# Regrouping the half-height cross matmuls and recoding ahead in a fused Perceiver layer

## The chip, the cores and the metric

The kernel runs on one core of a Trainium2 chip. The metric is the device time of one execution in microseconds (us). Before the change the median of three runs is 612.24 us (612.08 to 613.53).

## The reference, cut to what matters

```python
# x: (16, 64, 1024), ctx: (16, 1024, 1024), all float32
q1 = fake_quant(layernorm(x));  q2 = fake_quant(ctx)     # codes 0..255, scale 8/255, zero 128
x = x + q1 @ q2                                          # "cross": 64x1024 by 1024x1024 for each batch
x = x + out_proj(attention(layernorm(x)))                # qkv 1024 -> 3072, 32 heads of 32, rope, causal softmax
x = x + ffn(layernorm(x))                                # W.T plus 16 rank-16 updates, merged into one matrix
```

## The kernel before, in words

The 16 batches are worked in eight pairs of 2 x 64 = 128 rows. A pair's stage on the engines is `next_pair(i)`, and it does two things at once: the qkv projection, attention and output projection of pair i, and the cross product of pair i + 1. Pairs 0 and 1 have forms of their own (`first_pair`, and `next_pair` with `late`); pairs 2 to 6 run one body, and pair 7 has no cross left. No planner is at work: the order on each engine is written out by hand, every engine is strictly in order, and semaphores tie them together.

The cross of a pair reads 16 blocks of the context, called chunks here (8 of each batch, 128 x 1024 float32, 512 KB). A chunk passes through these hands:

- **SP** loads it (`load_chunk`, L679) into one of three float32 buffers, `slots`: `raw` 0, `raw` 1 and `lnt`. `lnt` is also where the normalised rows of norm2 stand until TensorE has turned them (`x_turn`), so a chunk can go there only afterwards (the wait on `s_xt`). Chunk c has slot c % 3. Each load waits for the coding of the chunk that had the slot.
- **ACT** codes it (`quantise`, L378) to bytes in the ring `code` of eight places, place c % 8. It waits for the load, and for TensorE (`s_cmm`) and POOL (`s_acc`) to be done with the chunk eight before.
- **POOL** adds the code words of all chunks of a pair, whose column sums TensorE needs for the zero point (`add_codes`, L811; two instructions for each chunk, for pairs 3 to 7).
- **DVE** casts the finished sums to float16 (`sums_as_f16`, L953), waiting for POOL's last chunk.
- **TensorE** multiplies. For pairs 3 to 7 ("tiled" in the code) `cross(i, *ks)` (L1417) uses the array as two halves of 64 columns, one for each batch: for each k two chunks, four matmuls of 512 columns, which go two at a time. `cross_shift` (L1429) does the same with the cast sums, eight matmuls. Then DVE adds both to the rows (`tiled_evac`, L959).

TensorE's order is in `next_pair(i, ahead)`. `qkv(i, j, between)` is one of six groups of 24 dense matmuls (k = 0 to 7, three for each k: L1353, L1354, L1355); the dictionary says what is put in after which k. In pairs 2 to 6 the cross of pair i + 1 stands in five places: `t(0, 1)` after qkv 2, k = 1; `t(2, 3)` after qkv 2, k = 7; `t(4, 5)` after qkv 3, k = 5; `t(6, 7)` after qkv 5, k = 0; and `shifted()` after qkv 5, k = 6. Around them stand the turns of q and k (`qk_turn`), the scores (L1508, two groups), the turns of the probabilities (`p_turn`), `values_due` and the values (L1534), and after qkv 5 the projection in four parts (L1547 to L1549), with `values` of the second half in the first part and `x_turn(i + 1)` between the second and the third.

ACT's order in `next_pair` mixes the 16 codings with the evacuations of turned blocks (`qk_evac` L394, `p_evac` L413, `a_high`, `x_high`, `c_high`) and the exponentials (L407). Chunks 0 and 1 of pair i + 2 are coded at the end of stage i, chunks 2 to 15 of pair i + 1 within stage i.

DVE's order in the second half of a stage is: `softmax_in(i, 2)`, `softmax_in(i, 3)` (L998, L1001, L1004), `v_sum(i, 0)` (L1021, which `values_due` waits for), `softmax_out(i, 2)` (L1010 to L1012), `sums_as_f16`, `softmax_out(i, 3)`, `tiled_evac` twice, `c_low(i, 0)` (L1028, which the projection waits for), `v_sum(i, 1)`, norm2 of pair i + 1.

SP's order (`next_set`) is: chunks 2 to 4 of pair i + 1, the store of a finished pair, chunks 5 to 15, and chunks 0 and 1 of pair i + 2.

## Time and profile before

| what | value |
|---|---|
| median of three runs | 612.24 us |
| the profiled execution's own time | 612.36 us |
| its span, first to last instruction | 610.3 us |
| TensorE matmul busy | 588.4 us, 96% of the span |
| DVE, ACT, POOL busy | 467.0, 292.8, 125.4 us |
| the chain that ended last | PE 79%, DVE 11%, SP queue 4%, DMA 3% |
| granted TensorE clock | 1.000 over the whole span |
| from HBM | 99.30 MB read |

The stages of pairs 2 to 6 lie between about 165 and 451 us of the span; the tables below take the stage of pair 4, which starts its qkv at 280.01 us and the next stage's at 337.25 us. A matmul of 512 columns is listed with 0.38 us, its time from start to end, but the next one starts 0.2155 us after it: matmuls overlap, and what counts for the length of a stage is the distance from start to start. "PE idle before" in a row appears only where the earlier matmul had ended, so short waits must be read from the starts too.

### The profile page before, as it was taken

What the parts mean: (1) busy time and instruction counts of PE and PEld (TensorE: products, weight loads), DVE (VectorE), ACT (ScalarE), POOL (GpSimd) and SP (SyncE); (2) the same over time, 40 slices, a digit from 0 to 9 for tenths busy, and PEclk for the clock granted to TensorE, in tenths of its full rate; (3) what the DMA queues carried; (4) which work ended last, traced back from release to release, by engine and by line L of the source; (5) the groups of instructions that cost most, each with busy time, mean ns of one, the idle gap of its engine ahead of it and who ended that gap; (6) DMA issues with size and microseconds to landing.
All of it is one profiled execution on the core that took longest, in us unless ns stands there. A gap on an engine that the chain in (4) does not pass through costs nothing.

```text
span 610.3 us, 12961 instructions
## 1 busy us (share of the span) xinstructions
PE 588.4 (96%) x4921; PEld 295.1 (48%) x4921; DVE 467.0 (77%) x931; ACT 292.8 (48%) x359; POOL 125.4 (21%) x173
## 2 busy tenths in 40 slices
PE   3889999999999999999999999999999999999998
PEld 1464455455545445544455445545445554444445
DVE  6999998778777866786677868678864789987751
ACT  5977695865456435634553464546331242210100
POOL 4000010000165234613541354345100000000000
PEclk9999999999999999999999999999999999999999
DMA  8999996861356255507531673265222025477541
GB/s 319 387 387 361 393 361 227 287 225 71 132 188 233 71 201 205 180 35 275 203 141 50 224 237 107 114 208 194 103 92 81 1 89 223 122 147 154 144 107 53
DMA packets 53698, 111.83 MB, mean 183 GB/s; under 512 B 18586, under 2 KB 18970, under 8 KB 53664
## 3 DMA queue, kind: packets, MB, share of 16 engines
q1 hardware_dynamic: 37744, 104.35, 49.4%
q10 hardware_dynamic: 15648, 6.48, 4.6%
q0 software_dynamic: 272, 0.55, 0.2%
q8 instruction: 21, 0.34, 0.2%
q14 instruction: 13, 0.11, 0.1%
HBM read 99.30 MB, written 8.39 MB: 176 GB/s over the span
## 4 chain that ended last, share of the span: by engine, by line
PE 79%; DVE 11%; SPq 4%; DMA 3%; issue 2%; ACT 1%; ACTq 0%; DVEq 0%
PE dense L1353 15%; PE dense L1355 15%; PE dense L1354 15%; PE turn L1344 5%; PE dense L1547 4%; PE dense L1549 4%; PE dense L1548 4%; DVE wq L941 4%; PE cross L1417 3%; PE score L1508 3%; PE dense L1563 2%; SPq L656 2%; DMA wq<-in_qkv_w 2%; PE cross L1402 2%; PE score L1534 2%
## 5 line engine op out<-in xcount | busy, mean ns | idle before, releaser
L1353 PE MATMUL dense<-wq,xn_h 128*128 128x512 f16 x400 | 152.2, 380 | 1.3 <-DMA xn_l<-spare 0.9
L1354 PE MATMUL dense<-wq,xn_h 128*128 128x512 f16 x400 | 151.6, 379 | 0.0
L1355 PE MATMUL dense<-wq,xn_l 128*128 128x512 f16 x400 | 151.6, 379 | 0.0
L811 POOL TENSOR_TENSOR acc<-code,acc 128x256 int32<-128x256 int32 x140 | 104.0, 773 | 114.1 <-ACT code L378 114.1
L378 ACT ACTIVATE code<-raw,cst,qc 128x1024 uint8<-128x1024 f32 x72 | 87.3, 1237 | 13.4 <-DMA raw<-in_ctx 12.9
L1353 PEld LDWEIGHTS dense<-wq,xn_h 128*128 128x128 f16 x400 | 39.0, 97 | 50.6 <-issue 14.0
L1355 PEld LDWEIGHTS dense<-wq,xn_l 128*128 128x128 f16 x400 | 39.1, 98 | 47.3
L1354 PEld LDWEIGHTS dense<-wq,xn_h 128*128 128x128 f16 x400 | 39.2, 98 | 34.9
L378 ACT ACTIVATE code<-lnt,cst,qc 128x1024 uint8<-128x1024 f32 x32 | 39.6, 1237 | 27.0 <-DMA lnt<-in_ctx 26.5
L998 DVE SCALAR_TENSOR_TENSOR at<-cst,score 128x512 f32<-128x512 f16 x24 | 16.4, 684 | 40.1 <-PE score L1508 40.1
L1547 PE MATMUL dense<-wo,rope 128*128 128x512 f16 x112 | 42.5, 379 | 0.8 <-DVE rope L1028 0.8
L1549 PE MATMUL dense<-wo,rope 128*128 128x512 f16 x112 | 42.4, 379 | 0.0
L1548 PE MATMUL dense<-wo,rope 128*128 128x512 f16 x112 | 42.4, 379 | 0.0
L407 ACT ACTIVATE at<-at 128x512 f32<-128x512 f32 x32 | 20.0, 628 | 37.5 <-DVE at L1004 37.4
L394 ACT ACTIVATE at<-turn 128x512 f32<-128x512 f32 x32 | 19.0, 593 | 37.2 <-PE turn L1344 24.0
L811 POOL TENSOR_TENSOR acc<-code,lw 128x256 int32<-128x256 int32 x20 | 11.6, 613 | 116.4 <-ACT code L378 116.4
L413 ACT ACTIVATE at<-turn 128x512 f32<-128x512 f32 x32 | 19.0, 592 | 32.3 <-PE turn L1344 32.2
L626 ACT ACTIVATE spare<-lnt 128x1024 f16<-128x1024 f32 x7 | 7.4, 1057 | 54.1 <-DVE lnt L1259 54.1
L1402 PE MATMUL cross<-code,q1t 128*128 128x512 f16 x96 | 28.3, 392 | 3.2 <-DVE xa L948 1.5
L984 DVE TENSOR_TENSOR rope<-dense,cst 128x512 f32<-128x512 f32 x32 | 22.0, 689 | 11.2 <-PE dense L1355 8.3
L990 DVE TENSOR_TENSOR rope<-rope 128x512 f32<-128x512 f32 x32 | 24.5, 766 | 1.4
L1035 DVE SCALAR_TENSOR_TENSOR xa<-dense,xa 128x512 f32<-128x512 f32 x16 | 11.0, 690 | 18.1 <-PE dense L1549 18.0
(225 smaller groups left out, 1036.3 us busy)
## 6 DMA issues: line engine op xcount, KB each, us to landing
raw<-in_ctx SPq DMA_DIRECT2D x72, 512.0 KB, 4.4
lnt<-in_ctx SPq DMA_DIRECT2D x32, 512.0 KB, 4.2
wo<-in_ctx SPq DMA_DIRECT2D x16, 512.0 KB, 8.8
wo<-in_qkv_w SPq DMA_DIRECT2D x12, 512.0 KB, 11.7
wq<-in_qkv_w SPq DMA_DIRECT2D x8, 512.0 KB, 11.9
x_scratch<-xa SPq DMA_DIRECT2D x8, 512.0 KB, 3.0
wq<-in_ctx SPq DMA_DIRECT2D x7, 512.0 KB, 11.7
wo<-in_out_w SPq DMA_DIRECT2D x7, 512.0 KB, 6.9
```

The source lines that it names most:

```text
L378: act.activation(low_bytes, src, ACT.Identity, scale=qc[:, 1:2], bias=z2).then_inc(s_u8, 1)
L811: ins = pool.tensor_tensor(sums[:, cols], words[:, cols], acc_from.to_broadcast([P, half]) if c < 2 else sums[:, cols], ALU.add)
L941: dve.scalar_tensor_tensor(lo, staged(j), WSC, hi, ALU.mult, ALU.subtract).then_inc(s_wlo, 1)
L990: dve.tensor_tensor(rope[:, 2 + j % 2, :], rope[:, 0, :], rope[:, 1, :], ALU.add).then_inc(s_qr, 1)
L1344: ins = pe.transpose(bank[:, k * P:(k + 1) * P], src[:, c:c + P], ident)
L1353: pe.matmul(bank[:, :], a_h[:, k, :], w_hi, start=(k == 0 and not started), stop=False)
L1354: pe.matmul(bank[:, :], a_h[:, k, :], w_lo, start=False, stop=False)
L1355: ins = pe.matmul(bank[:, :], a_l[:, k, :], w_hi, start=False, stop=(k == KC - 1 and not last))
L1402: ins = pe.matmul(X[n][:, :], lhs, code[:, c % RING, n * NT:(n + 1) * NT], start=(kc == 0), stop=(kc == KC - 1))
L1547: pe.matmul(D[n][:, :], c_h[:, k, :], wo_h[:, k, cols], start=(k == 0), stop=False)
L1548: pe.matmul(D[n][:, :], c_h[:, k, :], wo_l[:, k, cols], start=False, stop=False)
L1549: ins = pe.matmul(D[n][:, :], c_l[:, k, :], wo_h[:, k, cols], start=False, stop=(k == KC - 1))
```

## The change

- **TensorE**, stages of pairs 2 to 6: the cross of pair i + 1 stands in two places. `t(0, 1, 2, 3)` comes after qkv 2, k = 7; `t(4, 5, 6, 7)` and, right behind it, `shifted()` come after qkv 5, k = 1. The turn of q/k block 1 moves from k = 3 to k = 4 of qkv 2.
- **SP**: slots are given out otherwise: chunks 0 to 5 alternate between `raw` 0 and `raw` 1; from chunk 6 on all three go round, starting with `lnt`. So six chunks of pair i + 2 stand in SP's order before the end of a set, and only chunk 6 waits for `x_turn`. The store of the finished pair stands behind chunk 7.
- **ACT**: chunks 0 to 3 of pair i + 2 are coded in stage i, the first two between and behind the exponentials 2 and 3, the other two where chunks 0 and 1 were. Chunks 4 to 7 of pair i + 1 come first in the stage, in one row; chunks 8 to 15 are spread over the rest in a new order.
- **DVE**: the cast of the sums stands between `softmax_in(i, 2)` and `softmax_in(i, 3)`.
- Stage 1 (`late`) keeps its order on TensorE; on ACT it codes chunks 0 to 3 of pair 3 in the new places, and its loads follow the new slots.

```diff
@@ -112,7 +112,8 @@
         v_stage = [wq[:, :, n, 2 * DM:3 * DM].bitcast(F32) for n in range(KC)]
...
         slots = [raw[:, 0, :], raw[:, 1, :], lnt[:, :]]
-        uses = [len(range(n, CHUNKS, 3)) for n in range(3)]
+        slot_of = [c % 2 if c < 6 else (c - 4) % 3 for c in range(CHUNKS)]
+        uses = [slot_of.count(n) for n in range(3)]
         value_stage = [at_stage[:, 1, :, :], at_stage[:, 0, :, :], at_stage[:, 2, :, :], spare[:, :].rearrange("p (a n) -> p a n", a=2)] + o_stage[0:4]
...
         c_full = rope[:, 0:2, :].rearrange("p a n -> p (a n)").rearrange("p (m t) -> p m t", m=KC)
@@ -359,13 +360,13 @@
                     src = chunk0_stage(c)
...
                 else:
-                    n = c % 3
+                    n = slot_of[c]
                     src = slots[n].rearrange("p (a n) -> p a n", a=2)
...
                     else:
-                        act.wait_ge(s_slot[n], 16 * (uses[n] * (i - 2) + c // 3 + 1))
+                        act.wait_ge(s_slot[n], 16 * (uses[n] * (i - 2) + slot_of[:c].count(n) + 1))
                 taken = CHUNKS * i + c - (RING - 1)
...
                     act.wait_ge(s_cmm, taken)
@@ -498,39 +499,29 @@
                 def w(j):
...
                         weight_hi(j)
-                w(25)
-                q(2)
-                if not late:
-                    q(3, 4, 5)
-                a_high(i + 1, 0)
-                a_high(i + 1, 1)
                 if late:
+                    w(25)
+                    q(2)
+                    a_high(i + 1, 0)
+                    a_high(i + 1, 1)
                     q(3, 4)
...
                     w(27)
-                qk_evac(i, 0)
-                if not late:
-                    q(6)
-                q(7, 8)
-                w(28)
-                qk_evac(i, 1)
-                q(9)
-                w(29)
-                q(10)
-                if late:
-                    q(11)
-                exponent(i, 0)
-                if not isinstance(i, int) or i < PAIRS - 2:
+                    qk_evac(i, 0)
+                    q(7, 8)
+                    w(28)
+                    qk_evac(i, 1)
+                    q(9)
+                    w(29)
+                    q(10, 11)
+                    exponent(i, 0)
                     rows_after_next(i)
-                q(12 if late else 11)
-                exponent(i, 1)
-                qk_evac(i, 2)
-                if not late:
                     q(12)
-                q(13)
-                p_evac(i, 0)
-                if late:
+                    exponent(i, 1)
+                    qk_evac(i, 2)
+                    q(13)
+                    p_evac(i, 0)
                     p_evac(i, 1)
...
                     w(30)
@@ -539,20 +530,39 @@
                     v_evac(i, 0)
...
                 else:
-                    q(14)
+                    q(4, 5, 6, 7)
+                    a_high(i + 1, 0)
+                    a_high(i + 1, 1)
+                    qk_evac(i, 0)
+                    qk_evac(i, 1)
+                    q(8)
+                    exponent(i, 0)
+                    if not isinstance(i, int) or i < PAIRS - 2:
+                        rows_after_next(i)
+                    q(9, 10)
+                    exponent(i, 1)
+                    q(11)
+                    qk_evac(i, 2)
+                    q(12)
+                    p_evac(i, 0)
+                    q(13)
                     qk_evac(i, 3)
-                    q(15)
+                    q(14, 15)
                     p_evac(i, 1)
                 exponent(i, 2)
+                if more:
+                    quantise(i + 2, 0)
                 exponent(i, 3)
+                if more:
+                    quantise(i + 2, 1)
                 c_high(i, 0)
...
                 if more:
-                    quantise(i + 2, 0)
-                    quantise(i + 2, 1)
+                    quantise(i + 2, 2)
+                    quantise(i + 2, 3)
                 c_high(i, 1)
...
                 x_high(i + 1, 1)
@@ -655,7 +665,7 @@
                 if isinstance(i, int) and i == 0:
...
                     return
-                n = c % 3
+                n = slot_of[c]
                 if isinstance(i, int) and i == 1:
...
                         sp.wait_ge(s_xt, 2)
@@ -669,12 +679,14 @@
                         sp.wait_ge(s_u8, CHUNKS + c - 6)
...
                     return
-                if c == 2:
+                if c < 2:
+                    sp.wait_ge(s_u8, CHUNKS * i + c - (1 if isinstance(i, int) and i == 2 else 2))
+                elif c < 6:
+                    sp.wait_ge(s_u8, CHUNKS * i + c - 1)
+                elif c == 6:
                     sp.wait_ge(s_xt, 2 * i)
-                elif c >= 3:
+                else:
                     sp.wait_ge(s_u8, CHUNKS * i + c - 2)
-                else:
-                    sp.wait_ge(s_u8, CHUNKS * i - (0 if c == 0 else 2))
                 b, kc = block_of(i, c)
...
 
@@ -717,18 +729,18 @@
                 load_chunk(1, c)
...
                 load_weight(j)
-            load_chunk(2, 0)
-            load_chunk(2, 1)
+            for c in range(6):
+                load_chunk(2, c)
 
             def next_set(i, more):
-                for c in range(2, 5):
+                for c in range(6, 8):
                     load_chunk(i + 1, c)
                 store_x2(i - 1)
-                for c in range(5, CHUNKS):
+                for c in range(8, CHUNKS):
                     load_chunk(i + 1, c)
                 if more:
-                    load_chunk(i + 2, 0)
-                    load_chunk(i + 2, 1)
+                    for c in range(6):
+                        load_chunk(i + 2, c)
             next_set(1, True)
...
                 next_set(i, True)
@@ -1124,6 +1136,8 @@
                     cross_evac(i + 1, 0)
...
                 softmax_in(i, 2)
+                if not late:
+                    sums_as_f16(i + 1)
                 softmax_in(i, 3)
...
                 if late:
@@ -1134,7 +1148,6 @@
                 else:
...
                     softmax_out(i, 2)
-                    sums_as_f16(i + 1)
                     softmax_out(i, 3)
...
                     tiled_evac(i + 1, 1)
@@ -1733,7 +1746,7 @@
                 else:
...
                     qkv(i, 1, {3: [at(codes)], 5: [at(m, 0)], 6: [at(codes_turned, 0), at(qk_turn, i, 0)]})
-                    qkv(i, 2, {1: [at(t, 0, 1)], 3: [at(codes_turned, 1), at(qk_turn, i, 1)], 4: [at(m, 1)], 6: [at(middle_biases, i), at(scores, i, 0)], 7: [at(t, 2, 3)]})
+                    qkv(i, 2, {4: [at(codes_turned, 1), at(qk_turn, i, 1), at(m, 1)], 6: [at(middle_biases, i), at(scores, i, 0)], 7: [at(t, 0, 1, 2, 3)]})
                 late = isinstance(i, int) and i == 1
...
                     qkv(i, 3, {1: [at(c, 7)], 6: [at(turned, i, 1), at(qk_turn, i, 2)]})
@@ -1741,13 +1754,13 @@
                     qkv(i, 5, {1: [at(c, 10, 11)], 2: [at(c, 12, 13)], 3: [at(c, 14, 15), at(values_due, i, 0)], 4: [at(values, i, 0)],
...
                 else:
-                    qkv(i, 3, {2: [at(m, 2)], 5: [at(t, 4, 5)], 6: [at(turned, i, 1), at(qk_turn, i, 2)]})
+                    qkv(i, 3, {2: [at(m, 2)], 6: [at(turned, i, 1), at(qk_turn, i, 2)]})
                     if ahead:
...
                         qkv(i, 4, {1: [at(turned, i, 2), at(p_turn, i, 0), at(m, 3)], 4: [at(qk_turn, i, 3)], 6: [at(scores, i, 1)], 7: [at(p_turn, i, 1)]})
-                    qkv(i, 5, {0: [at(t, 6, 7)], 1: [at(m, 4)], 2: [at(m, 5)], 3: [at(values_due, i, 0)], 4: [at(values, i, 0)],
-                               6: [at(shifted), at(evacuated, i, 0), at(p_turn, i, 2)], 7: [at(p_turn, i, 3)]})
+                    qkv(i, 5, {1: [at(t, 4, 5, 6, 7), at(shifted), at(m, 4)], 2: [at(m, 5)], 3: [at(values_due, i, 0)], 4: [at(values, i, 0)],
+                               6: [at(evacuated, i, 0), at(p_turn, i, 2)], 7: [at(p_turn, i, 3)]})
                 project(i, 0, 0, {2: [at(values_due, i, 1)], 3: [at(values, i, 1)]})
...
```

## Rows read from the trace of the kernel before

**Rows 1.** The page: busy time by engine, and granted clock in 40 slices.

```profile
PE 588.4 (96%) x4921; PEld 295.1 (48%) x4921; DVE 467.0 (77%) x931; ACT 292.8 (48%) x359; POOL 125.4 (21%) x173
...
PEclk9999999999999999999999999999999999999999
```

**Rows 2.** Busy time by stretch: us; PE, PEld, DVE, ACT, POOL; clock; DMA.

```profile
274.10:331.40 57.30, 57.06 (x543) 28.47 (x541) 42.55 (x88) 29.55 (x36) 22.97 (x32) 1.00 0.47 165
```

**Rows 3.** Timeline of TensorE's matmuls, stage of pair 4, around `t(0, 1)`: start, duration.

```profile
292.76 0.38 PE L1355 MATMUL dense<-wq,xn_l 128*128 128x512 f16 x1
293.07 1.05 PE L1417 MATMUL cross<-code,q1t 128*64 128x512 f16 x8
294.05 0.39 PE L1353 MATMUL dense<-wq,xn_h 128*128 128x512 f16 x1
294.28 0.38 PE L1354 MATMUL dense<-wq,xn_h 128*128 128x512 f16 x1
```

**Rows 4.** Timeline of TensorE's matmuls, stage of pair 4, around `shifted()`.

```profile
321.94 0.38 PE L1355 MATMUL dense<-wq,xn_l 128*128 128x512 f16 x1
322.25 1.05 PE L1429 MATMUL cross<-acc,lw 128*64 128x512 f16 x8
323.23 0.66 PE L1344 MATMUL turn<-cst,at 128*128 128x128 f32 x4
323.72 0.38 PE L1353 MATMUL dense<-wq,xn_h 128*128 128x512 f16 x1
```

**Rows 5.** Timeline of TensorE's matmuls: scores 1, `values_due`, last turn, projection.

```profile
313.20 1.16 PE L1508 MATMUL score<-at 32*64 32x64 f32 x64
...
318.85 0.38 PE L1355 MATMUL dense<-wq,xn_l 128*128 128x512 f16 x1
319.31 0.39 PE L1353 MATMUL dense<-wq,xn_h 128*128 128x512 f16 x1
...
324.37 0.60 PE L1344 MATMUL turn<-cst,at 128*128 128x128 f32 x4
325.13 0.38 PE L1547 MATMUL dense<-wo,rope 128*128 128x512 f16 x1 [0.16 <-DVE rope L1028]
```

**Rows 6.** Timeline of DVE, stage of pair 4, second softmax half.

```profile
314.39 0.69 DVE L998 SCALAR_TENSOR_TENSOR at<-cst,score 128x512 f32<-128x512 f16 x1 [2.16 <-PE score L1508]
...
318.49 0.68 DVE L1021 SCALAR_TENSOR_TENSOR at<-dense,spare 128x512 f32<-128x512 f32 x1
...
320.65 0.69 DVE L953 CAST acc<-acc 128x2048 f16<-128x2048 uint16 x1
...
322.91 1.41 DVE L959 SCALAR_TENSOR_TENSOR xb<-cross,lw,xb 128x512 f32<-128x512 f32 x2
324.24 0.75 DVE L1028 SCALAR_TENSOR_TENSOR rope<-score,rope 128x256 f16<-128x256 f32 x2
```

**Rows 7.** Timelines of ACT and POOL: last evacuation, last coding, last four additions.

```profile
312.01 0.60 ACT L394 ACTIVATE at<-turn 128x512 f32<-128x512 f32 x1 [0.28 <-PE turn L1344]
312.71 1.24 ACT L378 ACTIVATE code<-raw,cst,qc 128x1024 uint8<-128x1024 f32 x1
...
309.13 6.43 POOL L811 TENSOR_TENSOR acc<-code,acc 128x256 int32<-128x256 int32 x8 [4.07 <-ACT code L378]
```

**Rows 8.** Timelines of DVE and POOL: DVE beside POOL's additions, POOL's next pair.

```profile
309.29 1.12 DVE L990 TENSOR_TENSOR rope<-rope 128x512 f32<-128x512 f32 x1
...
311.28 0.96 DVE L1012 TENSOR_TENSOR at<-at,ssum 128x512 f32<-128x512 f32 x1
...
326.91 2.32 POOL L811 TENSOR_TENSOR acc<-code,lw 128x256 int32<-128x256 int32 x4 [11.35 <-ACT code L378]
```

**Rows 9.** Loads of chunks (line L679), 216 to 446 us: issue to landing.

```profile
DMA to landing us min/median/max: 3.1/4.2/7.3
```

**Rows 10.** Timelines of ACT and TensorE, stage of pair 1: second evacuation, scores.

```profile
122.96 0.58 ACT L394 ACTIVATE at<-turn 128x512 f32<-128x512 f32 x1
...
125.41 1.16 PE L1508 MATMUL score<-at 32*64 32x64 f32 x64
```

## The prediction, made before the changed kernel ran

> **What bounds the kernel now.** First the page: TensorE is busy for 96% of the span, at a granted clock of 1.000 throughout [rows 1]. Then the busy time by stretch: the stage of pair 4 takes 57.2 us, 57.06 of 57.30 us of it busy on TensorE, while DVE has 42.6, ACT 29.6 and POOL 23.0 us [rows 2]; the stages of pairs 3 to 6 look the same, to 0.1 us. So only two things shorten a stage: fewer start-to-start distances on TensorE, and fewer of its waits. A list of waits shows hardly any, because a listed matmul lasts 0.38 us while the next could start after 0.2155. Both must be read from the starts in the timeline.
>
> **Term 1, the groups.** From the last dense matmul to the first behind `t(0, 1)` are 294.05 - 292.76 = 1.29 us [rows 3]. The dense matmul itself is 0.2155 of it, the eight half-height ones, two at a time, 4 x 0.2155 = 0.862; 0.21 is left, and the first dense matmul behind takes 0.23 for 0.2155. So going in and out costs 0.23 us a group: 0.095 in (293.07 - 292.76 - 0.2155), 0.135 out. For `shifted()`, with a turn behind it (0.49 for the usual 0.437), it is 0.095 + 0.12 + 0.05 = 0.26 [rows 4]. The change leaves two groups of five: it removes two at 0.23 and the shift's own at 0.26, 0.72 us a stage. The matmuls stay. Bounds: if a longer group paid at each k again, nothing; but two k's already stand in each group of rows 3 and pay once, so 0.72 is taken, and 0.78 if all three cost 0.26.
>
> The Trainium skill (TensorEngine Tiling (Array Packing), Tiling Modes) says that changing the tiling mode drains the engine, and gives no price; the rows supply one, and by that rule too the number of changes is what counts.
>
> **Term 2, the waits.** Two stand in the stage [rows 5]. `values_due` is after the dense matmul at 318.85: the next starts at 319.31, not 319.07, so 0.24 us, and DVE's `v_sum` (318.49 + 0.68 = 319.17) releases it [rows 6]. The projection could start 0.437 after the last turn, at 324.81, and starts at 325.13: 0.32 us, for `c_low` (ends 324.24 + 0.75 = 324.99). Together 0.56.
>
> Afterwards, counted from the start X of scores 1 (313.20 before):
> - DVE starts `softmax_in` 2 at X + 1.19, and its whole row of work to the end of `c_low` takes 10.60 (314.39 to 324.99) [rows 6]. The cast only changes its place in it. So the projection may start at X + 1.19 + 10.60 + 0.14 = X + 11.93.
> - TensorE, less its two waits, needs 324.81 - 0.24 - 313.20 = 11.37 from X to there. It gets `t(4, 5)` in this part (+ 0.862) and loses the shift's own group (- 0.26): X + 11.97. Slack 0.04, so the wait of 0.32 goes.
> - `v_sum` is a cast later (0.60), X + 6.57; TensorE comes to `values_due` at X + 5.87 + 0.862 + 0.862 = X + 7.59. The wait of 0.24 goes.
>
> **Term 3, new waits, the cast.** It now wants POOL's last sum at X + 1.19 + 2.06 = X + 3.25. ACT evacuates turn 3 at X - 1.19 and is free at X - 0.49 [rows 7]; then two codings follow where one did (1.13 + 1.24), ending at X + 1.88. POOL ends 1.61 behind the last coding now (315.56 against 313.95), so at X + 3.49. The cast waits 0.24, and with it all of DVE up to `c_low`: less the slack, 0.20 us a stage. The shift itself comes at X + 5.4, with the cast done at X + 4.2: no wait. Bounds: nothing if POOL is quicker, 1.3 if one more coding is behind.
>
> **Term 4, POOL beside DVE.** An addition of two SBUF tensors on DVE lengthens when POOL adds: L990 took 1.12 and L1012 0.96 us beside POOL, for 0.69 alone [rows 8]. POOL's chunk 0 of pair i + 2 now comes right behind the shift (X + 6.4 to 7.6) and chunk 1 at about X + 8.0, where DVE has `softmax_out` 2 and 3 (their L1012 at X + 7.7 and 9.3); before, both came at 326.91, after `c_low`. Bounds: zero if they miss each other, 2 x 0.43 if both are hit fully. I take 0.15, near the lower end, because both L1012 start just as POOL stops. The last stage (pair 6) has no pair i + 2, so none.
>
> The Trainium skill (SBUF — State Buffer, SBUF: two separate sides) has a rule against this part: DVE and POOL share a port pair that one instruction locks to its end, for DVE operations with two SBUF inputs. Rows 8 agree in direction; by the rule each hit L1012 waits for the rest of one addition, the upper bound above.
>
> **What costs nothing, and its cover.** The four codings at the head of a stage need their buffers sooner: chunks 4 and 5 are loaded once 2 and 3 are coded, at the end of the stage before, and ACT idles before `a_high` anyway. Coding 8 waits for TensorE to take chunk 0, now at qkv 2, k = 7 (about 299.8 in pair 4's times), and exponential 0 stands behind it; that is ready at about 300.4 and starts at about 301.0, 0.5 earlier than now. Exponential 3 stands behind the coding of chunk 0 of pair i + 2, which waits for chunk 8 to be consumed (X + 4.3) and ends at X + 5.5, before `softmax_in` 3 (X + 6.0). The turn of block 1, at k = 4, comes at 294.9 and needs DVE's rotation of 294.5: slack 0.3; its evacuation, no longer behind two codings, ends 1 us before scores 0. SP's store waits behind chunk 7's load, still 5 us before `out_base` wants it. The `x_turn` keeps its 1 us of slack.
>
> Stage 1 has only two slots for chunks 2 to 5. Walked by loads of 4.2 us [rows 9], ACT falls about 2 us behind there, and `qk_evac` 1, at 122.96 now, is done at about 125.2, where scores 0 stand at 125.41 [rows 10]: nothing, up to 1 us at worst.
>
> **The sum.** A stage gains 0.72 + 0.56 - 0.20 - 0.15 = 0.93 us; four of those and the last with 1.08 make 4.8. Less 0.1 for stage 1: 4.7. From the profiled execution, 612.36 (span 610.3 and about 2.1 around it, which stay), this leads to 607.7; the median is 0.12 lower: **607.5 us**.
>
> **Rivals.**
> - *A: no new wait shows.* POOL keeps up and the port is free: 1.28 x 5 = 6.4 us, 605.8. For it: terms 3 and 4 are each a quarter of a microsecond. Against: the cast is wanted before POOL's last sum by the sum of the rows. Chance 0.17.
> - *B: the gain is eaten (same).* New waits of 0.9 or more a stage take the place of the old: port hits of 0.86 and the cast together make 1.1, leaving 1.28 - 1.1 = 0.2 a stage, 1 us, 611.2. For it: DVE and TensorE are within 0.04 us at the projection, so whatever delays DVE is paid in full. Chance 0.12.
> - *C: loads bound the bunch (slower).* Chunks 8 to 15 are coded in 14 us behind one release, and each load waits for the coding three before. Coding 8 ends at 301.1; chunk 11 needs a load after it, chunk 14 another after 11: coding 15 ends at 301.1 + 2L + 3.8 at the earliest (two codings of 1.24, one of 1.13, 0.1 to issue each load), against the 313.8 of term 3 (X is 311.9 there). That holds up to L = 4.4; the median is 4.2, the longest 7.3 [rows 9]. At L = 5.5 it ends 2.1 late, the projection waits that much more, and a stage is 2.1 - 0.93 = 1.2 us longer than before: 618 us. It decides from about L = 4.9. Against: the loads of that stretch overlap only two or three at a time, and chunks 9 and 10 are there already. Chance 0.07.
> - *D: the groups are not what costs.* Were the 0.23 us a feature of how starts are recorded, only the waits would go: 0.21 a stage, 611. Against: the dense matmuls behind are really later. Chance 0.02.
> - The forecast, 606.2 to 609.6: 0.62.
>
> **How the numbers follow.** Some 0.3% (1.8 us) is what a measurement can tell from no change. Faster takes in the forecast and A, and a little of B: 0.84. Same: most of B, and D: 0.10. Slower: C less its mild cases, 0.06. The range reaches from A's centre with 0.4 below (term 1 at its upper bound) to 609.9, where the upper bound of term 4 and 0.3 more at the cast stand: 605.4 to 609.9; outside are B, C and D.
>
> **What would show it.** Right: stages of 56.2 to 56.5 us from start to start; two groups of L1417, each about 1.95 and (with L1429) 2.8 us; no gap at `values_due`; 0.2 to 0.5 us before the first L1547; the cast ending about X + 4.2 and starting straight behind POOL's last addition. L1012 of 0.9 us or more behind the shift shows term 4. Wrong: ACT waiting for `raw` or `lnt` between codings 11 and 15 by over 1 us (C), a projection wait of 1 us (B), or a group that costs more than 0.23 beyond its matmuls.

## The result, and the profile after

Over four runs each, the changed kernel takes 617.43 us (616.22 to 618.28) and the kernel before 612.45 (612.08 to 613.53): a ratio of 1.0077, 95% interval 1.0057 to 1.0096. It is slower by 5 us, where 607.5 (605.4 to 609.9) was forecast. The profiled execution took 618.22 us, its span 616.4. First three lines of the profile's page of the kernel after (busy time, the granted clock by slice, the chain that ended last; the first two as in [rows 1]):

```profile
PE 587.8 (95%) x4921; PEld 298.2 (48%) x4921; DVE 472.6 (77%) x931; ACT 291.9 (47%) x359; POOL 131.6 (21%) x173
...
PEclk9999999989999999999999999999999999999999
...
PE 59%; DVE 22%; DMA 7%; issue 6%; ACT 4%; POOL 1%; ACTq 0%; DVEq 0%; POOLq 0%; SPq 0%
```

TensorE has lost 20 points of the chain (79% before), DVE and DMA have gained 15, and the clock is below full speed in one slice of 40, the ninth (123 to 139 us). DVE and POOL are 5.6 and 6.2 us longer at work with the same instructions. The starts of the stages say where the time is (us from the first matmul of one qkv to the first of the next, profiled executions; the later rows are experiments):

| kernel | start of stage 1 | stages 1 to 6 |
|---|---|---|
| before | 105.43 | 59.87, 57.46, 57.25, 57.24, 57.24, 57.24 |
| after | 105.77 | **65.60**, 57.00, 57.56, 57.47, 57.56, 56.97 |
| after, store early (`a1_store`) | 104.88 | 60.20, 56.97, 56.97, 56.93, 57.54, 56.58 |
| before, store late (`b1_store_late`) | - | 63.99, 57.45, 57.23, 57.24, 57.33, 57.23 |
| `a1_store`, cast and shift late (`a4_cast_after_sum`) | - | 60.21, 56.36, 56.07, 56.08, 56.70, 56.07 |
| `a1_store`, POOL's work halved (`a6_half_pool`) | - | 59.86, 56.33, 55.96, 56.00, 56.56, 56.15 |
| before, four groups (`b2_four_groups`) | - | 59.87, 56.99, 56.76, 56.78, 56.76, 56.77 |
| before, three groups (`b3_three_groups`) | - | 59.86, 56.76, 56.55, 56.54, 56.54, 56.54 |
| the same, shift early, cast late (`b4_shift_at_values`) | - | 59.86, 56.31, 56.19, 56.30, 56.19, 56.07 |

There are two faults. Stage 1 is 5.7 us longer. And stages 2 to 6, forecast at 0.93 shorter each (the last 1.08), are 0.13 longer in sum. Part of that differs from execution to execution: `a1_store`, in which nothing of these stages was edited, took 285.0 us for them and the kernel after 286.6, and the last section shows one thing that it hangs on.

**Stage 1.** The list of waits of the kernel after (who waits, for whom; us in all, times, longest) names three waits that stand in no line of the same list of the kernel before:

```profile
DVE xa L916 <- DMA x_scratch<-xa: 5.5, 1, 5.5
...
DVE acc L965 <- POOL acc L823: 4.5, 5, 1.3
...
POOL acc L823 <- PE cross L1442: 8.2, 4, 2.3
```

L916 is `out_base(1)`: DVE overwrites `xa`, which holds the finished rows of pair 0, so it must wait until SP's store of them (L714) has landed. Before, the store and `out_base` stood so in the timelines of SP's queue and of DVE:

```profile
107.13 0.35 SPq L702 DMA_DIRECT2D x_scratch<-xa  x1
```

```profile
115.21 1.22 DVE L904 TENSOR_TENSOR xa<-xb,outb 128x1024 f32<-128x1024 f32 x1
```

The timelines of SP's queue, of DVE and of TensorE in the kernel after (start, length, line, tiles; the idle time before and its releaser):

```profile
93.22 19.43 SPq L691 DMA_DIRECT2D raw<-in_ctx  x6
113.09 0.51 SPq L691 DMA_DIRECT2D lnt<-in_ctx  x1
113.96 0.33 SPq L691 DMA_DIRECT2D raw<-in_ctx  x1
114.34 0.42 SPq L714 DMA_DIRECT2D x_scratch<-xa  x1
```

```profile
121.60 1.22 DVE L916 TENSOR_TENSOR xa<-xb,outb 128x1024 f32<-128x1024 f32 x1 [5.47 <-DMA x_scratch<-xa]
...
125.04 0.69 DVE L1002 TENSOR_TENSOR rope<-rope 128x512 f32<-128x512 f32 x1
```

```profile
121.99 0.38 PE L1368 MATMUL dense<-wq,xn_l 128*128 128x512 f16 x1
125.88 0.63 PE L1357 MATMUL turn<-cst,rope 128*128 128x128 f32 x4 [3.51 <-DVE rope L1002]
...
127.96 0.63 PE L1366 MATMUL dense<-wq,xn_h 128*128 128x512 f16 x1
128.39 0.63 PE L1367 MATMUL dense<-wq,xn_h 128*128 128x512 f16 x1
```

Read from the top: eight loads now stand in front of the store where five stood, and those of chunks 4, 5 and 7 each wait until ACT has coded the chunk that had the slot (chunk 7's, at 113.96, waits for the coding of chunk 4). So the store is issued at 114.34, not 107.13, and lands 7.24 us later, at 121.58; three loads are still in flight when it is issued. `out_base` ends at 122.82 (before, it started at 115.21), then come the rotations, and TensorE stands still for 3.7 us in front of the turn of q/k block 1 (125.88 - 121.99 - 0.2155). The matmul at 126.77 is already lengthened, and the eight from 127.11 on start 0.43 apart instead of 0.2155 (the last 0.41): the granted clock has gone from the upper to the lower of its levels, 2.4 to 1.2 GHz. The busy time by stretch has it as the mean clock (after the busy times of PE, PEld, DVE, ACT and POOL):

```profile
126.00:131.00 5.00, 5.00 (x19) 1.84 (x18) 2.09 (x2) 4.59 (x6) 0.00 (x0) 0.66 0.76 222
```

A mean of 0.66 is 0.34 short of full: 0.34 of 5 us is 1.7 us, on top of the stop.

**A steady stage**, pair 4's, TensorE (X, the start of scores 1, is 317.80):

```profile
317.80 1.16 PE L1521 MATMUL score<-at 32*64 32x64 f32 x64
...
321.38 1.92 PE L1430 MATMUL cross<-code,q1t 128*64 128x512 f16 x16
323.13 1.03 PE L1442 MATMUL cross<-acc,lw 128*64 128x512 f16 x8
324.09 0.39 PE L1366 MATMUL dense<-wq,xn_h 128*128 128x512 f16 x1
...
325.18 0.38 PE L1368 MATMUL dense<-wq,xn_l 128*128 128x512 f16 x1
...
326.14 0.39 PE L1366 MATMUL dense<-wq,xn_h 128*128 128x512 f16 x1 [0.58 <-DVE at L1033]
...
330.07 0.60 PE L1357 MATMUL turn<-cst,at 128*128 128x128 f32 x4
...
331.28 0.38 PE L1560 MATMUL dense<-wo,rope 128*128 128x512 f16 x1 [0.61 <-DVE rope L1040]
```

The group and its shift take 324.09 - 321.38 = 2.71 us. At `values_due` the next dense matmul starts at 326.14 and not at 325.40: 0.74 us. The projection starts 1.21 after the last turn, 0.77 more than the usual 0.437. So both waits stayed and grew, from 0.24 and 0.32 [rows 5]. In the five stages the wait at the projection is 0.75 to 0.78; the one at `values_due` is 0.07, 0.74, 0.74, 0.74 and 0.25. DVE, POOL and ACT show why:

```profile
319.00 0.69 DVE L1010 SCALAR_TENSOR_TENSOR at<-cst,score 128x512 f32<-128x512 f16 x1 [2.44 <-PE score L1521]
...
320.44 1.18 DVE L1016 TENSOR_TENSOR at<-at,smx 128x512 f32<-128x512 f32 x1
322.23 0.69 DVE L965 CAST acc<-acc 128x2048 f16<-128x2048 uint16 x1 [0.62 <-POOL acc L823]
...
324.28 1.13 DVE L1016 TENSOR_TENSOR at<-at,smx 128x512 f32<-128x512 f32 x1
325.33 0.68 DVE L1033 SCALAR_TENSOR_TENSOR at<-dense,spare 128x512 f32<-128x512 f32 x1
...
330.39 0.74 DVE L1040 SCALAR_TENSOR_TENSOR rope<-score,rope 128x256 f16<-128x256 f32 x2
```

```profile
318.79 3.41 POOL L823 TENSOR_TENSOR acc<-code,acc 128x256 int32<-128x256 int32 x4 [0.97 <-ACT code L379]
...
324.25 1.63 POOL L823 TENSOR_TENSOR acc<-code,lw 128x256 int32<-128x256 int32 x2 [2.05 <-PE cross L1442]
```

```profile
317.39 1.24 ACT L379 ACTIVATE code<-raw,cst,qc 128x1024 uint8<-128x1024 f32 x1 [0.18 <-DMA raw<-in_ctx]
...
318.94 1.24 ACT L379 ACTIVATE code<-lnt,cst,qc 128x1024 uint8<-128x1024 f32 x1 [0.31 <-DMA lnt<-in_ctx]
```

DVE's row from `softmax_in` 2 to the end of `c_low` takes 331.13 - 319.00 = 12.13 us, where [rows 6] gave 10.60. Three things of it are new: L1016 at 320.44 is 0.49 longer than its 0.69 (POOL adds beside it), the cast finds POOL unfinished (0.62), and L1016 at 324.28 is 0.44 longer: 1.55 together. The first two are one thing: the cast starts when POOL ends, at X + 4.43, and would do so with a short L1016 before it too.

### The profile page after: what moved, and what is told of

The parts are those of the page before. It is cut to its first block, busy times and chain, and to the rows that moved or that the text cites. A ratio compares the mean times of both kernels' runs of the same rounds, so it can differ in the third digit from the quotient of the medians.

```text
span 616.4 us, 12953 instructions
## 1 busy us (share of the span) xinstructions
PE 587.8 (95%) x4921; PEld 298.2 (48%) x4921; DVE 472.6 (77%) x931; ACT 291.9 (47%) x359; POOL 131.6 (21%) x173
## 4 chain that ended last, share of the span: by engine, by line
PE 59%; DVE 22%; DMA 7%; issue 6%; ACT 4%; POOL 1%; ACTq 0%; DVEq 0%; POOLq 0%; SPq 0%
PE dense L1366 11%; PE dense L1367 10%; PE dense L1368 10%; PE dense L1560 4%; DVE wq L953 4%; PE dense L1561 4%; PE dense L1562 4%; PE turn L1357 3%; DMA lnt<-in_ctx 3%; ACT code L379 3%; PE cross L1415 3%; PE dense L1576 2%; PE score L1521 2%; DVE smx L1013 1%; DMA raw<-in_ctx 1%
## 5 line engine op out<-in xcount | busy, mean ns | idle before, releaser
L823 POOL TENSOR_TENSOR acc<-code,acc 128x256 int32<-128x256 int32 x140 | 107.0, 792 | 150.2 <-ACT code L379 149.9
L379 ACT ACTIVATE code<-raw,cst,qc 128x1024 uint8<-128x1024 f32 x78 | 95.1, 1236 | 29.4 <-PE cross L1430 18.1
L379 ACT ACTIVATE code<-lnt,cst,qc 128x1024 uint8<-128x1024 f32 x26 | 32.2, 1238 | 7.5 <-DMA lnt<-in_ctx 7.5
L823 POOL TENSOR_TENSOR acc<-code,lw 128x256 int32<-128x256 int32 x20 | 14.9, 767 | 81.0 <-ACT code L379 72.8
L1024 DVE TENSOR_TENSOR at<-at,ssum 128x512 f32<-128x512 f32 x32 | 25.5, 798 | 1.1
```

The costliest lines, as they stand in the source:

```text
L379: act.activation(low_bytes, src, ACT.Identity, scale=qc[:, 1:2], bias=z2).then_inc(s_u8, 1)
L823: ins = pool.tensor_tensor(sums[:, cols], words[:, cols], acc_from.to_broadcast([P, half]) if c < 2 else sums[:, cols], ALU.add)
L1024: dve.tensor_tensor(p3, p3, ssum[:, g % 2, :].unsqueeze(2).to_broadcast([P, HPG, SEQ]), ALU.mult).then_inc(s_p, 1)
```

## The experiments

Theory S: the store's new place in set 1 makes the 5.7 us of stage 1. Theory P: in the steady stages the early cast, POOL's late end and POOL's additions beside DVE put `v_sum` and `c_low` later by what the groups and the old waits would have given. Rivals: T, the two slots (and ACT behind its loads) make stage 1 longer; G, fewer groups bring nothing. The kernels called `a` start from the kernel after, those called `b` from the kernel before.

**Only the store moved back (`a1_store`).** It is issued before chunk 4's load of pair 2; everything else is the kernel after.

```diff
-            for c in range(6):
+            for c in range(4):
+                load_chunk(2, c)
+            store_x2(0)
+            for c in range(4, 6):
                 load_chunk(2, c)
...
-                store_x2(i - 1)
+                if not isinstance(i, int) or i > 1:
+                    store_x2(i - 1)
```

> The changed kernel, with the store of pair 0's rows moved in front of the load of chunk 4 of pair 2 (stage 1 alone). Theory S (the store, queued behind the loads of chunks 5, 6 and 7, makes DVE's out_base wait 5.5 us, TensorE 3.7 us, and the clock fall): out_base of stage 1 starts at about 115.5, stage 1 takes 59.9 to 60.3 us instead of 65.6, the kernel 612.3 to 613.2 us. Rival T (two buffers for chunks 2 to 5 make ACT and the loads late in stage 1, whatever the store does): 2 us or more of the loss stays, 614.5 or more.

Measured: 611.40 us against 612.14, ratio 0.9989 (0.9979 to 0.9999): 5.4 us faster than the kernel after (1.0077 - 0.9989 of 612). The total is 0.9 us below the range expected. Stage 1 is back at 60.20, as expected. From SP's queue and DVE's timeline of this kernel:

```profile
106.58 0.35 SPq L714 DMA_DIRECT2D x_scratch<-xa  x1
```

```profile
115.23 1.22 DVE L920 TENSOR_TENSOR xa<-xb,outb 128x1024 f32<-128x1024 f32 x1
```

The store, issued with no load in flight, lands 2.63 us later, and `out_base` starts where it did before, without a wait. S holds; T is left with the 0.3 us by which 60.20 is above 59.87.

**Only the store moved, in the kernel before (`b1_store_late`).**

```diff
-                for c in range(2, 5):
+                before_store = 8 if isinstance(i, int) and i == 1 else 5
+                for c in range(2, before_store):
...
-                for c in range(5, CHUNKS):
+                for c in range(before_store, CHUNKS):
```

> The kernel before, with only this changed: in stage 1 the store of pair 0's rows stands behind the load of chunk 7, not of chunk 4. Theory S: the store is issued at about 113.9 and lands 3 to 7 us later, out_base starts at 118 to 121, the turn of block 1 is 0.5 to 4 us late, and up to 2 us more go to a lower clock: 613 to 618 us. Rival T: no change, 612.4.

Measured: 614.84 against 612.14, ratio 1.0042 (1.0028 to 1.0056). Its SP queue and DVE:

```profile
113.57 0.42 SPq L702 DMA_DIRECT2D x_scratch<-xa  x1
```

```profile
120.08 1.22 DVE L905 TENSOR_TENSOR xa<-xb,outb 128x1024 f32<-128x1024 f32 x1 [4.71 <-DMA x_scratch<-xa]
```

One moved store with nothing else costs 2.7 us in the median, half of the 5.4: here `out_base` starts 1.5 us earlier than in the kernel after, and TensorE's stop in front of the turn is 2.4 us, not 3.7. The executions fall into two sets: four between 613.75 and 614.88 with a mean granted clock of 1.000, two at 615.78 and 616.69 with 0.997. Only the one at 616.69 has a trace, and it shows the stop and the lower clock behind it. All six lie above the median of the kernel before, so the stop was most likely in all, though no trace shows it for the other five; the fall of the clock came in some only, and the two sets lie about 2 us apart. The kernel after has 0.997 in three of four executions, and 1.000 in its fastest, 616.22.

**Chunks 0 and 1 of pair i + 2 coded late (`a2_codes_late`).** From `a1_store`; in the steady stages the two codings go from beside exponentials 2 and 3 to behind `p_evac` 3.

```diff
-                if more:
+                if more and late:
                     quantise(i + 2, 0)
...
                 p_evac(i, 3)
+                if more and not late:
+                    quantise(i + 2, 0)
+                    quantise(i + 2, 1)
                 if more:
                     quantise(i + 2, 2)
```

> As a1_store, and in stages 2 to 5 chunks 0 and 1 of pair i + 2 are coded behind p_evac 3, with 2 and 3, instead of around the exponential 3. Theory P (POOL's addition of chunk 0 right behind the shift holds up L1016 of softmax_in 3, 1.13 us instead of 0.69): that L1016 takes 0.69, v_sum comes 0.44 earlier, the wait at values_due falls from 0.75 to 0.3, four stages lose 0.3 to 0.45 us each: 1.2 to 1.8 us less than a1_store. Rival (L1016 is long for another reason, or the freed time is lost again at the projection or because eight codings in a row delay x_high): within 0.4 us of a1_store.

Measured: 627.62, ratio 1.0251 (1.0233 to 1.0268), stages 2 to 5 of 59.8 to 61.2 us. As a time this missed altogether. One line of the stage of pair 4 bears on P, and is as theory P expected: with POOL's addition of chunk 0 gone from there, the second L1023 (L1016 in the kernel after) takes 0.69.

```profile
324.34 0.69 DVE L1023 TENSOR_TENSOR at<-at,smx 128x512 f32<-128x512 f32 x1
```

ACT and DVE show what took over:

```profile
335.71 1.24 ACT L379 ACTIVATE code<-raw,cst,qc 128x1024 uint8<-128x1024 f32 x1 [2.53 <-DMA raw<-in_ctx]
...
338.91 0.64 ACT L420 ACTIVATE rope<-score 128x256 f16<-128x256 f32 x2
```

```profile
339.31 0.75 DVE L1047 SCALAR_TENSOR_TENSOR rope<-score,rope 128x256 f16<-128x256 f32 x2 [3.39 <-ACT rope L420]
```

Chunk 2's load waits for the coding of chunk 0, and chunk 2 is coded right behind it: the load's time lies open on ACT, and `c_high`, behind it in the queue, holds the projection. With two slots for the first six chunks, the early codings of chunks 0 and 1 are what pays for chunks 2 and 3.

**TensorE's list of before in `a1_store` (`a3_five_groups`).** Meant to price the groups in the kernel after.

```diff
-                    qkv(i, 2, {4: [at(codes_turned, 1), at(qk_turn, i, 1), at(m, 1)], 6: [at(middle_biases, i), at(scores, i, 0)], 7: [at(t, 0, 1, 2, 3)]})
+                    qkv(i, 2, {1: [at(t, 0, 1)], 3: [at(codes_turned, 1), at(qk_turn, i, 1)], 4: [at(m, 1)], 6: [at(middle_biases, i), at(scores, i, 0)], 7: [at(t, 2, 3)]})
...
+                    qkv(i, 3, {2: [at(m, 2)], 5: [at(t, 4, 5)], 6: [at(turned, i, 1), at(qk_turn, i, 2)]})
...
+                    qkv(i, 5, {0: [at(t, 6, 7)], 1: [at(m, 4)], 2: [at(m, 5)], 3: [at(values_due, i, 0)], 4: [at(values, i, 0)],
+                               6: [at(shifted), at(evacuated, i, 0), at(p_turn, i, 2)], 7: [at(p_turn, i, 3)]})
```

> As a1_store, but TensorE's list for stages 2 to 7 is the one of before: five groups, the shift behind k = 6 of qkv 5. Slots, codings ahead and the early cast stay. Theory G (a group costs 0.23 to 0.26 us to go in and out): scores 1 start 33.2 us after the start of the stage's qkv (31.9 in the changed kernel), and as DVE is as late as before, counted from scores 1, the whole 0.7 to 1.3 us a stage is seen at the end: 3.5 to 6.5 us more than a1_store. Rival (the groups cost nothing, or what they cost is hidden behind DVE in any case): within 1 us of a1_store.

Measured: 633.07, ratio 1.0361 (1.0337 to 1.0386), far more than the groups can cost. Its TensorE row:

```profile
315.89 0.58 PE L1434 MATMUL cross<-code,q1t 128*64 128x512 f16 x2 [1.94 <-ACT code L379]
...
317.23 0.63 PE L1371 MATMUL dense<-wq,xn_h 128*128 128x512 f16 x1
317.66 0.63 PE L1372 MATMUL dense<-wq,xn_l 128*128 128x512 f16 x1
```

`t(4, 5)` at qkv 3, k = 5, comes before ACT, in its new order, has coded chunk 11. This stage, pair 4's, is 5.1 us longer than before: the stop is 2.1 (2.32 from start to start, less 0.2155), the lower clock behind it, with starts 0.43 apart, is 1.7, and the wait at `values_due` is 1.57 for 0.24. The two orders belong together, so this is no measurement of the groups.

**The groups alone, from the kernel before (`b2_four_groups`, `b3_three_groups`).** `b2` changes nothing but the place of `t(4, 5)`:

```diff
-                    qkv(i, 3, {2: [at(m, 2)], 5: [at(t, 4, 5)], 6: [at(turned, i, 1), at(qk_turn, i, 2)]})
+                    qkv(i, 3, {2: [at(m, 2)], 6: [at(turned, i, 1), at(qk_turn, i, 2)]})
...
-                    qkv(i, 5, {0: [at(t, 6, 7)], 1: [at(m, 4)], 2: [at(m, 5)], 3: [at(values_due, i, 0)], 4: [at(values, i, 0)],
+                    qkv(i, 5, {0: [at(t, 4, 5, 6, 7)], 1: [at(m, 4)], 2: [at(m, 5)], 3: [at(values_due, i, 0)], 4: [at(values, i, 0)],
```

> The kernel before with one edit on TensorE: the cross of chunks 8 to 11 (t(4, 5)) moves from qkv 3, k = 5 to the group of chunks 12 to 15 behind qkv 5, k = 0. Four groups for five, nothing else moves. Theory G (0.23 us a group, and TensorE's waits for v_sum and c_low go because TensorE has 0.86 us more to do there and DVE none): scores 1 start 32.1 us into the stage instead of 33.2, both waits (0.24 and 0.32) vanish, stages of 56.4 to 56.5 us for 57.24, 608.1 to 608.6 us in all. Rival (groups cost nothing): only the waits go, stages of 56.7, 609.4. Rival (DVE or POOL takes it back): 57.2, 612.

`b3` adds the joined `t(0, 1, 2, 3)`, the turn of block 1 at k = 4, and ACT's new order for chunks 6 to 15; slots, store, cast and the codings of pair i + 2 stay as before.

```diff
-                    qkv(i, 2, {1: [at(t, 0, 1)], 3: [at(codes_turned, 1), at(qk_turn, i, 1)], 4: [at(m, 1)], 6: [at(middle_biases, i), at(scores, i, 0)], 7: [at(t, 2, 3)]})
+                    qkv(i, 2, {4: [at(codes_turned, 1), at(qk_turn, i, 1), at(m, 1)], 6: [at(middle_biases, i), at(scores, i, 0)], 7: [at(t, 0, 1, 2, 3)]})
```

> As b2_four_groups, and chunks 0 to 3 join chunks 4 to 7 behind qkv 2, k = 7, as in the changed kernel, with ACT's order of the changed kernel from coding 6 on; slots, codings ahead (two) and the cast's late place as before. Theory: one group fewer again, 0.23 us a stage; the cast, late, does not wait for POOL: stages of 56.2 us, 607.0 to 607.8. Rival (eight codings in one bunch with their loads make something late even so): 57 us a stage or more, 611 or more.

Measured: `b2` 609.91 against 612.67, ratio 0.9961 (0.9947 to 0.9975); `b3` 608.72, ratio 0.9940 (0.9927 to 0.9954). From the start of a stage to X are 33.19 us before, 32.10 in `b2` (33.19 less the 0.862 of the matmuls that moved behind X, less 0.23) and 31.87 in `b3` (0.23 more): each group removed gives 0.23 us, as term 1 has it. In both the wait at `values_due` is gone (TensorE comes 0.86 later). The projection's 0.32 is still there, against the expectation, and the stages are about 0.3 longer than expected for it. Rival G is refuted. DVE in `b2`:

```profile
321.00 1.41 DVE L959 SCALAR_TENSOR_TENSOR xb<-cross,lw,xb 128x512 f32<-128x512 f32 x2 [0.18 <-PE cross L1429]
```

`tiled_evac` waits for the shift, which TensorE does just before the last two turns. So the projection's wait in `b2` is TensorE's own: shift, `tiled_evac`, `c_low`. In the kernel before, L959 starts 0.66 behind the shift too (322.91 - 322.25, [rows 6] and [rows 4]), as here (321.00 - 320.34), but DVE's own row of work would have let it start only 0.10 earlier: it starts 0.71 behind the L1012 at 322.20, where the row behind the L1012 at 320.04 started after 0.61.

**The cast late again, the shift behind the values (`a4_cast_after_sum`).** From `a1_store`.

```diff
                 softmax_in(i, 2)
-                if not late:
-                    sums_as_f16(i + 1)
                 softmax_in(i, 3)
...
                     v_sum(i, 0)
+                    sums_as_f16(i + 1)
...
-                    qkv(i, 5, {1: [at(t, 4, 5, 6, 7), at(shifted), at(m, 4)], 2: [at(m, 5)], 3: [at(values_due, i, 0)], 4: [at(values, i, 0)],
+                    qkv(i, 5, {1: [at(t, 4, 5, 6, 7), at(m, 4)], 2: [at(m, 5)], 3: [at(values_due, i, 0)], 4: [at(values, i, 0), at(shifted)],
```

> As a1_store, with the cast of the sums behind v_sum 0 instead of between softmax_in 2 and 3, and the shift behind the values of qkv 5, k = 4, instead of behind t(7). Theory C (the early cast stands 0.6 us for POOL's last addition and pushes POOL's next addition onto L1016): the cast does not wait, L1016 takes 0.69, v_sum ends 6.0 us behind scores 1 instead of 7.6 to 8.2, no wait at values_due, at most 0.2 at the projection: stages of 56.1 to 56.4, 607.5 to 608.8 us. Rival (DVE is late because of its own work or the port in any case): stages of 56.9 or more, 611 or more.

Measured: 607.18 against 612.67, ratio 0.9917 (0.9904 to 0.9931), by the ratios 4.4 us better than `a1_store`, and a little better than expected. In four of the five steady stages, which take 56.07 to 56.36, neither wait is over 0.07. The stage of pair 5 takes 56.70, and there POOL and DVE stand so:

```profile
375.03 2.77 POOL L827 TENSOR_TENSOR acc<-code,lw 128x256 int32<-128x256 int32 x4 [5.05 <-PE cross L1445]
```

```profile
375.06 1.13 DVE L1028 TENSOR_TENSOR at<-at,ssum 128x512 f32<-128x512 f32 x1
```

POOL starts 0.03 us ahead, DVE's row (L1012 of before, the place of term 4) takes 1.13 for 0.69, and the projection waits 0.61. P holds: with cast and shift off the road to `v_sum`, the stage of pair 4 is 1.17 shorter than before, where groups and waits were to give 1.28.

**POOL at half its work (`a6_half_pool`).** From `a1_store`; for chunks 2 to 15 only the first half of the columns is added, so the output lacks the column sums of the rest in the zero-point term.

```diff
-                for h in range(2):
+                for h in range(2 if c < 2 else 1):
```

> As a1_store, but POOL adds only the first half of the columns of chunks 2 to 15 (the sums of the other half lack them, so the cross of pairs 3 to 7 is shifted by wrong sums there). Theory C: POOL ends its last addition about 0.8 us sooner and meets DVE's two-input operations half as often: the cast's wait goes, v_sum comes about 1 us sooner, the waits at values_due and at the projection fall from 0.2 to 0.75 and 0.77 to under 0.3 together: stages of 56.0 to 56.4, 608 us or less. Rival (the cast waits for the loads and codings, not for POOL): stages as in a1_store, 611.

Measured: 606.55, ratio 0.9901 (0.9886 to 0.9916). The early cast and the shift stay where the change put them, and by the ratios 5.4 us still go. The wait at `values_due` is gone in all five steady stages, and the cast waits for POOL in one only. The projection's wait, 0.63 to 0.78 in `a1_store`, is 0.38, 0.00, 0.06, 0.61 and 0.20. What hurts is POOL's late end and its additions beside DVE, not the place of the cast as such.

**The best version (`b4_shift_at_values`).** `b3` with the cast behind `v_sum` 0 and the shift behind the values (the edit is shown against the kernel before):

```diff
                     v_sum(i, 0)
+                    sums_as_f16(i + 1)
...
-                    qkv(i, 5, {0: [at(t, 6, 7)], 1: [at(m, 4)], 2: [at(m, 5)], 3: [at(values_due, i, 0)], 4: [at(values, i, 0)],
-                               6: [at(shifted), at(evacuated, i, 0), at(p_turn, i, 2)], 7: [at(p_turn, i, 3)]})
+                    qkv(i, 5, {0: [at(t, 4, 5, 6, 7)], 1: [at(m, 4)], 2: [at(m, 5)], 3: [at(values_due, i, 0)], 4: [at(values, i, 0), at(shifted)],
+                               6: [at(evacuated, i, 0), at(p_turn, i, 2)], 7: [at(p_turn, i, 3)]})
```

> As b3_three_groups (slots, codings ahead and stage 1 as before, two groups of eight chunks), with the cast behind v_sum 0 and the shift behind the values of qkv 5, k = 4. Theory L (the 0.32 us left at the projection in b2 and b3 is the chain shift, tiled_evac, c_low, which TensorE's own late shift starts): the shift is three dense groups earlier, that wait goes, and its own way in and out is mostly shared with the values: stages of 56.0 to 56.1 us, 606.0 to 606.8 us in all, and no stage of 56.7 as in a4_cast_after_sum, since POOL's chunk 0 comes only behind the last p_evac. Rival (the wait at the projection is DVE's own work since scores 1): it stays at 0.2 to 0.3, stages of 56.3 or more, 607.5 or more.

Measured: 606.46 against 612.87, ratio 0.9893 (0.9877 to 0.9910), better than both kernels, with the slots, the store and the codings of pair i + 2 of the kernel before. At `values_due` and at the projection no wait is over 0.13 us. The stages, 56.07 to 56.31, are up to 0.2 longer than expected.

## Why the prediction was wrong

**The step that failed** is in "what costs nothing": "SP's store waits behind chunk 7's load, still 5 us before `out_base` wants it". In a steady stage it holds: in pair 4's the store is issued at 287.00 and lands at 289.95, and `out_base` starts at 296.25. Set 1 has no such 5 us: the store waits behind loads that wait for codings, and before it had 2.6 us to spare: issued 107.13, landed 5.5 later at 112.6, `out_base` at 115.21. Now it is issued 7.2 later and takes 1.7 longer to land. The sentence on stage 1 ("nothing, up to 1 us at worst") walked ACT's codings, where 0.3 us did appear, and never SP's queue. The price is 5.4 us in the runs; in the profiled stage it is 3.7 of stop and 1.7 of clock. No rival had it either; rival C's figure of 618 is near the result by accident, for loads in the steady stages took 3.2 to 6.5 us, 4.3 in the median, below C's 4.9.

**Term 1** (0.72 a stage) is right. `b2` and `b3` show two of the three groups, at 0.23 each; the third, the shift's, has no run of its own, but the stage of pair 4 adds up with it to 0.01 (below).

**Term 2** (0.56) is wrong for the kernel as changed, because of terms 3 and 4. TensorE came to `values_due` at X + 7.60, as forecast (7.59), but `v_sum` ended at X + 8.21, not 6.57. The projection was forecast at X + 11.97 and came at X + 13.48: 1.51 late, 0.74 and 0.77. One premise was incomplete besides: the old 0.32 was laid to DVE's own row of work alone, while in `b2`, and by 0.10 in the kernel before, DVE waits there for the late shift.

**Term 3**, the early cast, had the right mechanism and is the term that was mis-sized most in the steady stages. POOL was to end at X + 3.49 and ended at X + 4.40. Of the 0.9, ACT's last coding is 0.50 (it ends at X + 2.38, not 1.88, with 0.18 and 0.31 spent on loads that were priced at nothing) and POOL 0.41 (2.02 behind the last coding, not 1.61). The cast was wanted at X + 3.25 and started at X + 4.43: 1.18 late, where 0.24 was forecast.

**Term 4** (0.15) looked for the collision at L1012 (now L1024) behind the shift. It came earlier, on the two L1016: POOL's last two chunks beside the one (0.49), and chunk 0 of pair i + 2, which the earlier shift releases, beside the other (0.44). The first of these costs nothing by itself, since the cast behind it waits for POOL in any case. Two stages of `a1_store` show it, first pair 3's, where that row is lengthened, then pair 5's, where it is not and the cast waits longer:

```profile
256.56 1.10 DVE L1020 TENSOR_TENSOR at<-at,smx 128x512 f32<-128x512 f32 x1
...
258.29 0.69 DVE L969 CAST acc<-acc 128x2048 f16<-128x2048 uint16 x1 [0.62 <-POOL acc L827]
...
370.46 0.69 DVE L1020 TENSOR_TENSOR at<-at,smx 128x512 f32<-128x512 f32 x1
...
372.45 0.69 DVE L969 CAST acc<-acc 128x2048 f16<-128x2048 uint16 x1 [1.30 <-POOL acc L827]
```

The second is paid in full. Rival B named this sum of port and cast, but priced it at 1.1 a stage with a chance of 0.12. The waits cost 1.51: 57.24 - 0.72 - 0.56 + 1.51 = 57.47, the measured stage of pair 4.

So stages 2 to 6 missed by 4.9 us and stage 1 by 5.6, and the profiled execution by 618.22 - 607.7 = 10.5; what lies before and behind these stages adds nothing. `a4` and `a6` change POOL's late end and the lengthened rows together, but the stages of `a1_store` part them. Where the second L1020 takes 0.69 (pairs 3 and 4), the projection still starts 1.0 later than X + 11.97: that is POOL's late end. Where it takes 1.00 (pair 5), the projection starts 1.6 later: 0.31 of the further 0.6 is the lengthened row, and the cast starts another 0.3 later. Why POOL takes 0.41 longer behind the last coding stays open.

## What to carry to other kernels

A moved DMA must be followed in every stage that runs the code, the first one above all: list what is now ahead of it in its queue and what each of those waits for. Before an instruction is put earlier on a busy engine, check that its own input is there earlier too, and what its end releases on an engine beside which its successors take longer. And where a wait looks like one engine's load, see whether that engine has itself waited just before: a lengthened instruction in front of a wait that would last anyway costs nothing.

## What the runs showed of the hardware

- **Which of DVE and POOL starts first sets the length of DVE's row.** In `a1_store` the same pair of instructions met both ways. DVE's timeline and POOL's, first the stage at 260 us and then that at 374:

```profile
260.33 0.69 DVE L1020 TENSOR_TENSOR at<-at,smx 128x512 f32<-128x512 f32 x1
...
374.49 1.00 DVE L1020 TENSOR_TENSOR at<-at,smx 128x512 f32<-128x512 f32 x1
```

```profile
260.37 1.69 POOL L827 TENSOR_TENSOR acc<-code,lw 128x256 int32<-128x256 int32 x2 [2.12 <-PE cross L1446]
...
374.34 1.63 POOL L827 TENSOR_TENSOR acc<-code,lw 128x256 int32<-128x256 int32 x2 [1.92 <-PE cross L1446]
```

With DVE ahead by 0.04 us its row takes 0.69 and the stage 56.97; with POOL ahead by 0.15 it takes 1.00 and the stage 57.54. The Trainium skill (SBUF — State Buffer, SBUF: two separate sides) says that whoever starts first gets the shared ports for its whole instruction. The order agrees; the delay does not quite: 0.31 to 0.49 us, where one of POOL's two additions is listed with about 0.8 (1.63 for two). POOL's two additions take 1.69 in the one order and 1.63 in the other, so on its side the order makes no difference that these rows show.
- **A stop can cost more than its length.** In the profile of the kernel after, the matmuls behind a stop of 3.7 us ran at the lower clock for 1.7 us more than their due. Shorter stops did it too: 2.4 us in `b1_store_late`, and 2.1 us in `a3_five_groups` (the rows at 317.23 above). But the same stop of 2.1 us one stage earlier in that run, at 255.19, has none behind it, and by the mean clock one of the four executions of the kernel after and four of the six of `b1_store_late` had none. Behind the waits of 0.7 us in the steady stages of the kernel after no slice of its page shows less than full clock.
- **A store among loads lands later.** The same store of 512 KB landed 2.63 us after its issue with no load in flight (`a1_store`), 5.5 with three in flight, of which one was just landing (before), 6.5 with two (`b1_store_late`) and 7.24 with three (after); in all four further loads were issued before it landed. How much of the difference is the traffic and how much the order in the queue is not shown.
